# The gated residual of a local-global attention stage, on GpSimd instead of VectorE, with the normalisation one step later

## The chip, the cores and the metric

One core of a Trainium2 chip runs the whole program in one launch. The metric is device microseconds of that core, as a median of runs. Engines: TensorE (PE in the profile; PEld its weight loads), VectorE (DVE), ScalarE (ACT), GpSimd (POOL), SyncE (SP).

## The reference

A decoder of twelve sublayers on x of shape 8 x 256 x 256, each followed by x = layernorm(x + sublayer(x)). The fourth one, a local attention and a global one (over rows compressed four to one) mixed by a gate, is what the change touches. Shortened, it is:

```python
def _L1_attn_ref(x, ...):
    local_x = x[..., :LD]                                   # LD = 128, HH = 8 heads of 16
    lq, lk, lv = split(local_x @ w_lqkv + b_lqkv)
    local_out = _causal_attn(heads(lq), heads(lk), heads(lv)) @ w_lproj + b_lproj
    compressed = x.reshape(Bx, Tc, R * C) @ w_comp + b_comp  # R = 4 rows are one
    gq, gk, gv = split(compressed[..., LD:] @ w_gqkv + b_gqkv)
    global_out = _causal_attn(heads(gq), heads(gk), heads(gv)) @ w_gproj + b_gproj
    global_out = jnp.repeat(global_out, R, axis=1)
    combined = jnp.concatenate([local_out, global_out], axis=-1)
    gate_w = jax.nn.softmax(combined @ w_gate + b_gate, axis=-1)
    return jnp.concatenate([gate_w[..., 0:1] * local_out, gate_w[..., 1:2] * global_out], axis=-1)
...
x = _layernorm(x + _L1_attn_ref(x, ...), axis=-1)
```

## The kernel before

x is held twice in SBUF: x_tok has tokens on the partitions (16 tiles of 128 tokens x 256), x_feat has features on the partitions and feeds the matmuls. A stage is one block in which each engine has its own instruction stream, executed in order; semaphores join them. Everything is f32.

local_global_attention (L1834) works on four groups of two batches (GROUPS = 4, 512 tokens). A group has twelve units of two heads each: eight of local attention (four a batch, 256 tokens; blocks of 128x128 and 128x256 scores) and four of global attention (128 compressed rows, one block a head). The engines follow one hand-written list of steps: `for t in range(STEPS)` runs in each stream, and at_step(t - k, 12, GROUPS) places a piece of work k steps behind the start of its group. Unit u has its scores and minima at step u + 4, its turned probabilities at u + 5, its products at u + 6. So the end of group g (its projection and gate, steps 22 to 28 behind its start) runs beside the units of group g + 1; for group 3 nothing runs beside it.

What each stream does around the gate of group g, by the steps behind the group's start:

- TensorE, in this order in each step: turn_out (L2005; every other step), project_qk (L1909), scores (L1950), turn_back (L2015), compress (L1932, at 6 of a later group; it waits until the x_feat of the group two before it is stored), turn_x (L2043, at 27 and 28, which is batch_turn, L857: four 128x128 transposes of the normalised x_tok), project_v (L1920), output (L2026, at 22 and 23), products (L1983), turn_probs (L1970). The scores of unit u wait for the minima of unit u - 1 and for the normalised output of an earlier pair (out_stored).
- VectorE, in this order in each step: lows (L2204, the masked minima of one unit, side_added), gate_logits (L2250, at 22 and 23), normalise (L2224, every other step), gate_tops (at 24), store_v (L2185), store_probs (L2217), store_back (L2243), gate_shares (L2270, at 25: three small operations), then residual and batch_statistics of the first batch (at 25) and of the second (at 26), then batch_normalise of the first (at 26) and of the second (at 27).
- ScalarE, in this order: batch_store (L867, at 27 and 28: the turned x into x_feat), store_qk (L2079), store_out, store_probs, gates (L2143), store_back, exps (L2110).
- GpSimd: masks at the start, then only batch_power (L841), the power -1/2 of the variances, a 128x2 operation a batch. SyncE issues only loads at the start of the stage.

residual (L2276) is four scalar_tensor_tensor operations a batch, one for each tile of tokens and each half of the features (local, global), x = both * gate + x, where `both` is the ungated output (L2255) and gate a 128x1 column. batch_statistics (L826) is two bn_stats of 128x256, two bn_aggr and one tensor_scalar.

Of the kernel before, what the change touches and what calls it, by code (L numbers as in the profile page):

```python
# [24 lines left out]
P = 128  # L25
# [76 lines left out]
def signals_of_odd_turns(sem):  # L102
# [58 lines left out]
    S.row_loaded_1 = S.masked = sem("odd_row_loaded_1_or_masked")  # L161
    S.row_loaded_2 = sem("odd_row_loaded_2")
    S.row_loaded_3 = sem("odd_row_loaded_3")
# [1670 lines left out]
def local_global_attention(nc, K):  # L1834
# [3 lines left out]
    UNITS, QUADS, EVENTS = GROUPS * SPAN, GROUPS * SPAN // 2, GROUPS * 3  # L1838
    STEPS = (GROUPS - 1) * SPAN + 29
    SM, TB, X, YA, YV, YX = (0, 1), (2, 3), 4, 5, 6, 7  # L1840
# [36 lines left out]
    with turn(nc, K) as block:  # L1877
# [10 lines left out]
        @block.gpsimd  # L1888
        def _(p):
            nc.gpsimd.memset(vh, 0.0).then_inc(S.masks_done, 1)  # L1890
            nc.gpsimd.memset(hide, 0.0).then_inc(S.masks_done, 1)
            nc.gpsimd.memset(gvh, 0.0).then_inc(S.masks_done, 1)
            p.wait_ge(S.masks_done, 3)
            nc.gpsimd.memset(vh[:, :, :, :, HD:HD + 1], 1.0)
            nc.gpsimd.memset(gvh[:, :, HD:HD + 1], 1.0)
            for at in (0, 2 * P, 3 * P):
                ins = nc.gpsimd.affine_select(out=hide[:, at:at + P], in_=hide[:, at:at + P], compare_op=ALU.is_ge,
                                              fill=-MASKED, base=0, pattern=[[-1, P]], channel_multiplier=1)
            ins.then_inc(S.masks_done, 1)
            p.wait_ge(S.masks_done, 4)  # L1900
            paired = hide[:, 3 * P:3 * P + P // 2]
            nc.gpsimd.affine_select(out=paired, in_=paired, compare_op=ALU.is_gt, fill=-MASKED, base=P // 2,
                                    pattern=[[0, P // 2]], channel_multiplier=-1).then_inc(S.masks_done, 1)
            for b in range(B):
                batch_power(nc, p, K, tail, b)

        @block.tensor
        def _(pe):
# [140 lines left out]
            for t in range(STEPS):  # L2049
# [13 lines left out]
                for i in range(2):  # L2063
                    if (g := at_step(t - 27 - i, SPAN, GROUPS)) is not None:
                        turn_x(2 * g + i)
# [12 lines left out]
        def _(a):  # L2078
# [70 lines left out]
            for t in range(STEPS):  # L2149
                for i in range(2):  # L2150
                    if (g := at_step(t - 27 - i, SPAN, GROUPS)) is not None:
                        batch_store(nc.scalar.copy, a, K, 2 * g + i, YX)
# [19 lines left out]
        def _(v):  # L2172
# [97 lines left out]
            def gate_shares(g):  # L2270
                v.wait_ge(S.hid_done, g + 1)
                then(nc.vector.tensor_reduce(total, gate, AX.X, ALU.add))
                then(nc.vector.reciprocal(total, total))
                then(nc.vector.tensor_tensor(gate, gate, spread(total, 2), ALU.mult))

            def residual(b):  # L2276
                for n in range(2):
                    for c in range(2):
                        x = K.x_tok[:, 2 * b + n, c * P:(c + 1) * P]
                        i = 2 * (b % 2) + n  # L2280
                        ins = nc.vector.scalar_tensor_tensor(out=x, in0=both[:, b % 2, n, c * P:(c + 1) * P],
                                                             scalar=gate[:, i, c:c + 1], in1=x, op0=ALU.mult, op1=ALU.add)
                ins.then_inc(S.residual_done, 1)

            for t in range(STEPS):
# [20 lines left out]
                for i in range(2):  # L2306
                    if (g := at_step(t - 25 - i, SPAN, GROUPS)) is not None:
                        residual(2 * g + i)
                        batch_statistics(nc, v, K, tail, 2 * g + i)
                for i in range(2):  # L2310
                    if (g := at_step(t - 26 - i, SPAN, GROUPS)) is not None:
                        batch_normalise(nc, v, K, tail, 2 * g + i)
# [2793 lines left out]
```

## Time and profile before

| what | value |
|---|---|
| median of 3 runs | 2589.14 us (2584.22, 2589.14, 2590.63) |
| the profiled execution, its own time | 2594.83 us |
| its span, first to last instruction | 2593.1 us |
| mean granted TensorE clock | 0.924 of full |
| busy share PE / PEld / DVE / ACT / POOL | 86% / 62% / 54% / 41% / 28% |
| the stage of the change, about | 545 to 759 us of the span |
| the four gates' last operation (L2274) starts at | 627.49, 675.38, 725.54, 750.15 us |

The profiled execution took 1.7 us more than its span, and 5.7 us more than the median of the runs. Busy shares are means over twelve stages with different limits, so they say little of one stage; the timeline around the gates is what shows who waits for whom. In timeline rows a group of equal instructions is merged into one, its second number is the time from the start of the first to the end of the last, and what stands in brackets is how long the engine was idle before it, and who ended that.

### The profile page before, as it was taken

How to read it: one execution, taken by the hardware profiler on the slowest of the kernel's cores; microseconds unless marked ns; L12 is line 12 of the kernel's file. 1: busy time of each engine (PE TensorE's matmuls, PEld its weight loads, DVE VectorE, ACT ScalarE, POOL GpSimd, SP SyncE). 2: the span in 40 equal slices, each digit the busy share in tenths (PEclk: the TensorE clock that was granted, in tenths of full speed). 3: DMA queues.
4: the chain of work that ended last, by engine and by line, in shares of the span. 5: the costliest groups of instructions: out<-in, count | busy, mean ns of one | idle time of the engine just before them, and what ended most of it. 6: DMA issues, size and time to landing. Idle time of an engine off the chain costs nothing. (4 is left out here: it accounts for less than half of the span.)

```text
span 2593.1 us, 37797 instructions
## 1 busy us (share of the span) xinstructions
PE 2218.9 (86%) x12776; PEld 1613.4 (62%) x12776; DVE 1409.6 (54%) x4103; ACT 1060.4 (41%) x2653; POOL 723.4 (28%) x738
## 2 busy tenths in 40 slices
PE   7993599888869959995699799687899799899898
PEld 5772377665547648883388566354465587465687
DVE  3664122256658947757133567544777443777455
ACT  3542111135516620055034166343567543567532
POOL 2323311110004414411634200363534200534111
PEclk9995799979959979996899899899999899999899
DMA  9132211085000010030254301401000000000000
GB/s 235 43 146 103 75 51 44 14 168 43 1 7 1 1 43 1 19 135 7 92 151 129 128 18 29 169 1 33 1 1 1 1 1 1 1 1 1 21 25 21
DMA packets 112237, 127.32 MB, mean 49 GB/s; under 512 B 46515, under 2 KB 100021, under 8 KB 110256
## 3 DMA queue, kind: packets, MB, share of 16 engines
q1 hardware_dynamic: 103312, 103.91, 14.9%
q0 software_dynamic: 8736, 20.99, 2.2%
q8 instruction: 106, 1.74, 0.3%
q14 instruction: 83, 0.68, 0.1%
HBM read 79.93 MB, written 47.90 MB: 49 GB/s over the span
## 5 line engine op out<-in xcount | busy, mean ns | idle before, releaser
L461 PE MATMUL bank<-weights,work 128*128 128x256 f32 (+5 forms) x1768 | 452.4, 393 | 18.8 <-DVE weights L2552 8.1
L461 PE MATMUL bank<-work,weights 128*128 128x256 f32 (+2 forms) x1552 | 392.8, 404 | 19.3 <-DVE work L4794 12.1
L461 PEld LDWEIGHTS bank<-weights,work 128*128 128x128 f32 (+2 forms) x1768 | 318.4, 191 | 101.1 <-issue 49.6
L461 PEld LDWEIGHTS bank<-work,weights 128*128 128x128 f32 x1552 | 293.5, 194 | 91.0 <-DVE work L4794 16.2
L845 POOL TENSOR_TENSOR work<-work,minus_half 128x2 f32<-128x2 f32 x96 | 69.3, 722 | 705.9 <-DVE work L838 705.9
L461 PE MATMUL bank<-weights,x_feat 128*128 128x512 f32 (+2 forms) x576 | 213.6, 505 | 14.8 <-ACT weights L4398 9.1
L870 ACT COPY x_feat<-bank 128x512 f32<-128x512 f32 x80 | 46.6, 585 | 301.8 <-PE bank L862 301.8
L461 PEld LDWEIGHTS bank<-weights,x_feat 128*128 128x128 f32 x576 | 107.4, 199 | 71.8 <-issue 45.9
L4422 ACT ACTIVATE work<-work 128x128 f32<-128x128 f32 (+1 forms) x256 | 137.1, 545 | 0.2
L461 PE MATMUL bank<-x_feat,weights 128*128 128x256 f32 (+3 forms) x400 | 117.7, 472 | 22.1 <-PEq L247 15.2
L1785 DVE TENSOR_TENSOR work<-bank,work 128x384 f32<-128x384 f32 (+1 forms) x64 | 31.4, 491 | 190.6 <-ACT work L1703 190.6
L461 PE MATMUL bank<-weights 128*128 128x256 f32 (+1 forms) x560 | 128.5, 386 | 1.6 <-ACT weights L4441 0.9
L4494 DVE CUSTOM_DVE_ANT_0 work<-bank,work 128x128 f32<-128x128 f32 (+1 forms) x256 | 76.2, 355 | 77.9 <-PE bank L4313 77.5
L461 PEld LDWEIGHTS bank<-weights 128*128 128x128 f32 x560 | 106.8, 196 | 17.0 <-ACT weights L4441 1.4
L461 PE MATMUL bank<-work 128*128 128x256 f32 (+3 forms) x390 | 90.4, 367 | 29.9 <-ACT work L3014 7.8
L461 PEld LDWEIGHTS bank<-x_feat,weights 128*128 128x128 f32 (+1 forms) x400 | 78.4, 214 | 47.6 <-issue 21.1
L862 PE MATMUL bank<-ident,x_tok 128*128 128x128 f32 x320 | 57.4, 311 | 44.9 <-DVE x_tok L853 42.8
L4264 POOL TENSOR_TENSOR work<-work,minus_half 128x8 f32<-128x8 f32 x32 | 52.4, 1637 | 151.3 <-DVE work L4527 151.3
L461 PEld LDWEIGHTS bank<-work 128*128 128x128 f32 (+2 forms) x390 | 66.6, 200 | 44.5 <-issue 12.7
L1603 POOL DMA_INDIRECT rows_back<-work x40 | 38.9, 971 | 196.2 <-DVE work L1793 196.2
L4804 DVE SCALAR_TENSOR_TENSOR work<-bank,weights,work 128x256 f32<-128x256 f32 x96 | 45.5, 481 | 81.3 <-ACT work L4742 80.8
L853 DVE TENSOR_SCALAR x_tok<-x_tok,work 128x256 f32<-128x256 f32 x192 | 80.6, 462 | 14.4 <-POOL work L845 14.2
(461 smaller groups left out, 4503.6 us busy)
## 6 DMA issues: line engine op xcount, KB each, us to landing
weights<-in_weights SPq DMA_DIRECT2D x1, 12296.0 KB, 33.1
weights<-in_weights SPq DMA_DIRECT2D x1, 9360.0 KB, 25.7
weights<-in_weights SPq DMA_DIRECT2D x1, 8488.0 KB, 23.1
work<-rows_in SPq DMA_DIRECT2D x62, 129.0 KB, 2.2
rows_in<-ident SPq DMA_DIRECT2D x2, 3968.0 KB, 43.1
weights<-rows_back SPq DMA_DIRECT2D x8, 768.0 KB, 4.9
work<-rows_in SPq DMA_DIRECT2D x8, 645.0 KB, 4.2
rows_in<-ident SPq DMA_DIRECT2D x2, 2560.0 KB, 33.5
```

The lines of the kernel that those rows point to most:

```text
L461: ins = nc.tensor.matmul(out, lhsT, rhs, start=(i == 0), stop=(i == len(pairs) - 1))
L845: nc.gpsimd.tensor_tensor(t.rstd[:, n, :], t.rstd[:, n, :], K.minus_half[:, 0:2], ALU.pow).then_inc(K.S.rstd_done, 1)
L853: ins = nc.vector.tensor_scalar(x, x, t.mv[:, b % 2, i, 0:1], t.rstd[:, b % 2, i:i + 1], ALU.subtract, ALU.mult)
L862: ins = nc.tensor.transpose(K.bank[bank][:, (2 * k + i) * P:(2 * k + i + 1) * P], K.x_tok[:, 2 * b + i, k * P:(k + 1) * P], K.ident[:])
L870: copy(K.x_feat[:, :, b * L:(b + 1) * L], K.bank[bank][:, :].rearrange("p (k t) -> p k t", k=KT)).then_inc(K.S.xT_stored, 1)
L1603: nc.gpsimd.indirect_dma_start(K.rows_back, bass.IndirectOffsetOnAxis(ap=to, axis=0), y[:, r, :], None, bounds_check=TOP * T - 1, oob_is_e ...
L1785: nc.vector.tensor_tensor(hT[:, q % 2, m, 0:n], K.bank[2 * (at % 2) + 1][:, 0:n], gelu[:, at % 2, 0:n], ALU.mult).then_inc(S.inner_stored, 1)
L4264: nc.gpsimd.tensor_tensor(rk, norm[:, 1, :], K.minus_half[:, 0:H], ALU.pow).then_inc(S.rk_done, 1)
L4422: ins = nc.scalar.activation(probs[:, u % 3, s, at:at + width], probs[:, u % 3, s, at:at + width], ACT.Exp, bias=bias[:, u % 2, i, s:s + 1 ...
L4494: ins = nc.vector.tensor_tensor_reduce(probs[:, u % 3, s, at:at + width], K.bank[SM[s]][:, at:at + width], seen[:, at:at + width], 1.0, -3 ...
L4804: nc.vector.scalar_tensor_tensor(out=hid[rows, b % 2, f, :], in0=K.bank[n % RING][rows, 0:L], scalar=W["b1"][rows, layer, f:f + 1], in1=ge ...
```

## The change

GpSimd gets the residual: for each batch one multiplication of `both` by the gate (128x512 elements, the gate a broadcast operand of 128x4), a wait for itself, and one addition to x_tok (128x512). It waits for gate_stored, a new signal of the last operation of gate_shares. Its power operations of a group stand behind both residuals of that group. On VectorE batch_statistics goes from steps 25 and 26 to 26 and 27, batch_normalise from 26 and 27 to 27 and 28; turn_x on TensorE and batch_store on ScalarE go from 27 and 28 to 28 and 29.

```diff
--- before.py
+++ after.py
@@ -159,7 +159,7 @@
     S.slots_loaded_2 = S.xc_stored = sem("odd_slots_loaded_2_or_xc_stored")
     S.row_loaded_0 = S.sq_stored = sem("odd_row_loaded_0_or_sq_stored")
     S.row_loaded_1 = S.masked = sem("odd_row_loaded_1_or_masked")
-    S.row_loaded_2 = sem("odd_row_loaded_2")
+    S.row_loaded_2 = S.both_scaled = sem("odd_row_loaded_2_or_both_scaled")
     S.row_loaded_3 = sem("odd_row_loaded_3")
     S.row_loaded_4 = sem("odd_row_loaded_4")
     S.row_loaded_5 = sem("odd_row_loaded_5")
@@ -1836,7 +1836,7 @@
     H, HD = 8, 16
     SPAN, LEAD = 12, 4
     UNITS, QUADS, EVENTS = GROUPS * SPAN, GROUPS * SPAN // 2, GROUPS * 3
-    STEPS = (GROUPS - 1) * SPAN + 29
+    STEPS = (GROUPS - 1) * SPAN + 30
     SM, TB, X, YA, YV, YX = (0, 1), (2, 3), 4, 5, 6, 7
 
     qT, kz = A(2, L), A(2, 2, L)
@@ -1901,8 +1901,22 @@
             paired = hide[:, 3 * P:3 * P + P // 2]
             nc.gpsimd.affine_select(out=paired, in_=paired, compare_op=ALU.is_gt, fill=-MASKED, base=P // 2,
                                     pattern=[[0, P // 2]], channel_multiplier=-1).then_inc(S.masks_done, 1)
-            for b in range(B):
-                batch_power(nc, p, K, tail, b)
+
+            def residual(b):
+                i = b % 2
+                parts = both[:, i, :, :].rearrange("p n (c d) -> p (n c) d", c=2)
+                p.wait_ge(S.gate_stored, b // 2 + 1)
+                nc.gpsimd.tensor_tensor(parts, parts, gate[:, 2 * i:2 * i + 2, :].rearrange("p n c -> p (n c)").unsqueeze(2)
+                                        .broadcast_to([P, 4, P]), ALU.mult).then_inc(S.both_scaled, 1)
+                p.wait_ge(S.both_scaled, b + 1)
+                x2 = K.x_tok[:, 2 * b:2 * b + 2, :]
+                nc.gpsimd.tensor_tensor(x2, x2, both[:, i, :, :], ALU.add).then_inc(S.residual_done, 1)
+
+            for g in range(GROUPS):
+                residual(2 * g)
+                residual(2 * g + 1)
+                batch_power(nc, p, K, tail, 2 * g)
+                batch_power(nc, p, K, tail, 2 * g + 1)
 
         @block.tensor
         def _(pe):
@@ -2061,7 +2075,7 @@
                 if (g := at_step(t - 6, SPAN, GROUPS)) is not None:
                     compress(g)
                 for i in range(2):
-                    if (g := at_step(t - 27 - i, SPAN, GROUPS)) is not None:
+                    if (g := at_step(t - 28 - i, SPAN, GROUPS)) is not None:
                         turn_x(2 * g + i)
                 for i in range(2):
                     if (g := at_step(t - 4 * i - 1, SPAN, GROUPS)) is not None:
@@ -2148,7 +2162,7 @@
 
             for t in range(STEPS):
                 for i in range(2):
-                    if (g := at_step(t - 27 - i, SPAN, GROUPS)) is not None:
+                    if (g := at_step(t - 28 - i, SPAN, GROUPS)) is not None:
                         batch_store(nc.scalar.copy, a, K, 2 * g + i, YX)
                 if (g := at_step(t - 8, SPAN, GROUPS)) is not None:
                     store_global(g)
@@ -2271,16 +2285,7 @@
                 v.wait_ge(S.hid_done, g + 1)
                 then(nc.vector.tensor_reduce(total, gate, AX.X, ALU.add))
                 then(nc.vector.reciprocal(total, total))
-                then(nc.vector.tensor_tensor(gate, gate, spread(total, 2), ALU.mult))
-
-            def residual(b):
-                for n in range(2):
-                    for c in range(2):
-                        x = K.x_tok[:, 2 * b + n, c * P:(c + 1) * P]
-                        i = 2 * (b % 2) + n
-                        ins = nc.vector.scalar_tensor_tensor(out=x, in0=both[:, b % 2, n, c * P:(c + 1) * P],
-                                                             scalar=gate[:, i, c:c + 1], in1=x, op0=ALU.mult, op1=ALU.add)
-                ins.then_inc(S.residual_done, 1)
+                nc.vector.tensor_tensor(gate, gate, spread(total, 2), ALU.mult).then_inc(S.gate_stored, 1)
 
             for t in range(STEPS):
                 if (u := at_step(t - LEAD, 1, UNITS)) is not None:
@@ -2304,11 +2309,10 @@
                 if (g := at_step(t - 25, SPAN, GROUPS)) is not None:
                     gate_shares(g)
                 for i in range(2):
-                    if (g := at_step(t - 25 - i, SPAN, GROUPS)) is not None:
-                        residual(2 * g + i)
+                    if (g := at_step(t - 26 - i, SPAN, GROUPS)) is not None:
                         batch_statistics(nc, v, K, tail, 2 * g + i)
                 for i in range(2):
-                    if (g := at_step(t - 26 - i, SPAN, GROUPS)) is not None:
+                    if (g := at_step(t - 27 - i, SPAN, GROUPS)) is not None:
                         batch_normalise(nc, v, K, tail, 2 * g + i)
```

## Rows read from the trace of the kernel before

**Rows 1.** Windows: stretch, its us, busy PE, PEld, DVE, ACT, POOL, PEclk, DMA, GB/s.

```profile
633.00:636.00 3.00, 2.10 (x11) 1.41 (x12) 1.69 (x11) 0.85 (x2) 0.78 (x1) 0.50 0.00 0
```

**Rows 2.** Timeline, first gate: start us, us, engine line op out<-in [idle before <-releaser].

```profile
627.49 0.17 DVE L2274 TENSOR_TENSOR work<-work 128x8 f32<-128x8 f32 x1
...
627.70 1.14 DVE L2281 SCALAR_TENSOR_TENSOR x_tok<-work,x_tok 128x128 f32<-128x128 f32 x4
...
628.87 0.75 DVE L831 BATCH_NORM_STATS2 work<-x_tok 128x6 f32<-128x256 f32 x2
...
629.94 0.17 DVE L838 TENSOR_SCALAR work<-work 128x2 f32<-128x2 f32 x1
...
630.30 0.28 DVE L2212 CUSTOM_DVE_ANT_0 work<-bank,work 128x128 f32<-128x128 f32 x1
...
630.51 0.28 DVE L2222 COPY work<-bank 128x128 f32<-128x128 f32 x1
...
630.70 0.41 PE L2011 MATMUL bank<-ident,work 128*128 128x128 f32 x2 [2.55 <-issue]
...
633.90 1.09 PE L862 MATMUL bank<-ident,x_tok 128*128 128x128 f32 x4 [2.38 <-DVE x_tok L853]
...
634.37 0.35 DVE L2238 TENSOR_TENSOR work<-bank,work 128x64 f32<-128x64 f32 x2
...
637.82 1.56 PE L1967 MATMUL bank<-work 32*128 32x128 f32 x8
...
639.60 0.60 PE L862 MATMUL bank<-ident,x_tok 128*128 128x128 f32 x4
...
642.28 1.52 ACT L2115 ACTIVATE work<-work 128x128 f32<-128x128 f32 x4
...
643.86 0.88 PE L1979 MATMUL bank<-ident,work 128*128 128x128 f32 x6 [0.99 <-ACT work L2115]
...
645.52 3.92 PE L461 MATMUL bank<-x_feat,weights 128*128 128x128 f32 x16
```

**Rows 3.** Timeline, same columns, second gate (first row) and third gate.

```profile
681.79 1.09 PE L862 MATMUL bank<-ident,x_tok 128*128 128x128 f32 x4 [2.38 <-DVE x_tok L853]
...
725.54 0.17 DVE L2274 TENSOR_TENSOR work<-work 128x8 f32<-128x8 f32 x1
...
735.35 1.09 PE L862 MATMUL bank<-ident,x_tok 128*128 128x128 f32 x4
...
740.07 0.47 PE L2023 MATMUL bank<-ident,work 128*128 128x128 f32 x1 [0.53 <-DVE work L2238]
```

**Rows 4.** Timeline, same columns, fourth gate and the end of the stage.

```profile
750.15 0.17 DVE L2274 TENSOR_TENSOR work<-work 128x8 f32<-128x8 f32 x1
...
754.98 0.73 DVE L853 TENSOR_SCALAR x_tok<-x_tok,work 128x256 f32<-128x256 f32 x2
...
755.86 1.09 PE L862 MATMUL bank<-ident,x_tok 128*128 128x128 f32 x4 [9.64 <-DVE x_tok L853]
```

**Rows 5.** GpSimd elsewhere: timeline of two dependent operations, one line's min/median/max ns.

```profile
1820.55 1.26 POOL L4267 TENSOR_TENSOR work<-work 128x512 f32<-128x512 f32 x1
1821.96 1.04 POOL L4271 TENSOR_TENSOR work<-work 128x512 f32<-128x512 f32 x1
...
L3911 POOL TENSOR_TENSOR x_tok<-x_tok,weights x8: 1257/1446/1530, 1662.6 to 1764.7; 128x512 f32<-128x512 f32 x8
```

**Rows 6.** Timeline, another stage: L4076 beside a GpSimd operation, and alone.

```profile
1662.57 1.26 POOL L3911 TENSOR_TENSOR x_tok<-x_tok,weights 128x512 f32<-128x512 f32 x1
1662.68 1.70 DVE L4076 TENSOR_TENSOR work<-weights,work 128x512 f32<-128x512 f32 x1
...
1665.22 0.69 DVE L4076 TENSOR_TENSOR work<-weights,work 128x512 f32<-128x512 f32 x1
```

**Rows 7.** Timeline: the scores behind the gate logits, first and third gate.

```profile
621.92 0.49 PE L1967 MATMUL bank<-work 32*128 32x128 f32 x4 [1.43 <-DVE work L2238]
...
717.63 0.79 PE L1967 MATMUL bank<-work 32*128 32x128 f32 x4 [2.29 <-DVE work L2238]
```

## The prediction

> **What bounds the kernel now.** I read the page first: TensorE is the busiest engine over the span, but that is a mean over twelve stages. I then took the timeline around each gate, following TensorE's idle time and what ended it; after that the windows, for the granted clock, and last GpSimd's groups in other stages, for prices.
>
> In the first gate the gate is ready at 627.66 us (627.49 + 0.17). VectorE then runs the residual and the statistics of one batch before the minima of unit 22 may start, near 630.1. TensorE stood idle 2.55 us for those minima; after its scores it stood idle 2.38 us more for the normalised x_tok, because turn_x stands ahead of products in its queue [rows 2]. The trace calls the first of the two "issue", but what it waited for is side_added, and it started 0.12 us after the last of the minima (630.30 + 0.28). The granted clock then was at 0.50, the lower level (1.2 GHz) [rows 1], and the scores of unit 24 took 1.56 us. The second gate repeats this, with 2.38 us ahead of turn_x [rows 3]. The third has no scores to feed after its first steps, and the fourth nothing beside it: there the chain gate, residual, statistics, power, normalisation, turning is the path itself, and TensorE was idle 9.64 us before it [rows 4]. So the stage has two bounds: in gates 1 and 2 VectorE's order, which holds TensorE; at the end, the length of the chain.
>
> **Part by part.** *Removed from VectorE:* 4 operations a batch, 1.14 us [rows 2], eight times. *Added to GpSimd:* two operations a batch. The stage has no such row. The nearest are two dependent 128x512 operations of another stage: 1.26 us with two full operands, then after a 0.15 us wait for itself 1.04 us with a broadcast operand, as the gate is here [rows 5]. So a residual is 1.04 + 0.15 + 1.26 = 2.45 us, two are 4.90, and the batch's power operation stands behind both. *Bounds:* additions to x_tok took 1.257 to 1.530 us [rows 5]; with 1.53 for both operations a residual is 3.2 us, and with 1.04 for both 2.2. I keep 2.45, from the nearest forms. The wait for the gate gets 0.1 us (TensorE started 0.12 us behind the minima that it waited for).
>
> *The step moved.* First gate, instruction by instruction. GpSimd: first residual 627.76 to 630.21, second to 632.66, both powers behind it. VectorE: minima 22 (0.49) to 628.15, store_probs (0.28) to 628.45 [rows 2]; it then waits for GpSimd until 630.25. Behind that wait stand the minima 23, the normalised output and store_probs, and TensorE's scores 24 wait for them. Statistics, from the start of bn_stats to the end of the last one, are 628.87 to 630.11, that is 1.24 us: to 631.49. Minima 23 to 631.98; the normalised output, about 0.6 (its second half is 0.35), to 632.6; store_probs to 632.9 [rows 2]; statistics of the second batch to 634.1 (its residual is in at 632.66, so no wait); normalisation 0.73 [rows 4] to 634.85. TensorE meanwhile does the scores 23, products 21, turned probabilities 22 and project_qk with nothing in their way, until some 630.9; scores 24 at 632.65; turn_x at 634.97 (0.12 us behind the normalisation).
>
> In the kernel before, the turning that follows scores 24 started at 639.60, and the turned probabilities of unit 24 at 643.86, with ScalarE's copy, store_qk, stores and exponentials between them (exponentials from 642.28) [rows 2]: 4.26 us. The same sequence stands behind the turning in the new kernel, so the turned probabilities start at 634.97 + 4.26 = 639.23. **Gain of the gate: 643.86 - 639.23 = 4.6 us.** The second turning comes at about 637.6, in TensorE's idle time. The compression at 645.52 needs both turnings stored; it moves to some 641, behind the second copy. From there on TensorE is the bound, so the gain stays. The second gate is the same: 4.6.
>
> Third gate: gate ready at 725.71; the same walk puts the first normalisation's end at 732.9 and the turning at 733.0 to 734.1 at the low clock. Products and turned probabilities (some 1.2) end at 735.3, store_probs, store_back and normalisation (0.28 + 0.28 + 0.73) at 736.65; the second turning, 1.09 us, at 737.85 (before: 736.44) [rows 3]. Before, the products of the last unit also came behind it, but waited for a copy of their probabilities that now is long there; I get 739.9 for the turning of the last output against 740.07. **Gain 0.2 us.**
>
> Fourth gate, all on the path: gate at 750.32, both residuals in at 750.32 + 0.1 + 4.90 = 755.32; VectorE's statistics of the second batch stand ahead of the first normalisation, so that ends at 755.32 + 0.04 + 1.24 + 0.73 = 757.33, against 754.98 + 0.73 = 755.71 before [rows 4]. The two turnings and copies follow as before. **Loss 1.6 us.** The step that the loops are longer, the semaphore under a second name and the wait saved behind gate_shares cost nothing: no engine has work in them. SyncE's and GpSimd's queues are passed by no DMA of this stage. The cover of GpSimd's work is the minima and stores of units 22 and 23; in the fourth gate it is gone, which is the 1.6.
>
> **Sum:** -4.6 - 4.6 - 0.2 + 1.6 = -7.8 us: 2594.8 becomes 2587.0 by the profiled execution, which is 5.7 above the median of the runs; on the median, 2589.1 - 7.8 = 2581.3. In general each 0.1 us on the mean price of a GpSimd operation (1.225 with the wait) costs 0.4 us in each of the four gates, 1.6 in all.
>
> A rule against the change is in the Trainium skill, "GPSIMD Engine Reference", section Engine selection: elementwise work on a tile belongs on VectorE, GpSimd being about twice slower with two inputs. By the rule, twice VectorE's 0.69 us of a 128x512 operation [rows 6] is 1.38 for each, the mean with the wait 1.455, and the sum -7.8 + 3.7 = -4.1. Of the rows, 1.26 is near it and 1.04, the broadcast form, is not.
>
> **The rivals.**
>
> A. The walk as above, -7.8, with some 1.5 to either side for its small terms. 0.50.
>
> B. The clock. In the third gate the granted clock also fell: there TensorE had idled 2.29 us for the logits, and the scores took 0.79 us where the same ones of the first gate, behind 1.43 us of idle, took 0.49. From those scores to the last gate operation it was 725.54 - 717.63 = 7.91 us, against 627.49 - 621.92 = 5.57 [rows 2, 3, 7]. If earlier work shifted by 9 us keeps it high there, 2.3 more are gained: -10.1. For: the falls follow recent idle time, which changes. Against: those 2.29 us of idle stay. 0.20.
>
> C. The clock falls in the gates all the same. TensorE's new idle stretches are about 1.7 and 1.1 us, with 1.2 of work between; the rows have one case behind 1.43 with the clock up and one behind 2.29 with it down [rows 7]. At the low level the turning is 1.09 for 0.60 and scores 1.56 [rows 2], and about 2 us of each gain go: -3.6. 0.16.
>
> D. GpSimd and VectorE hold each other up. L4076 took 1.70 us beside a GpSimd operation and 0.69 alone [rows 6]. If the statistics did so, each would end about 1 us later: -7.8 + 2 x 4 x 0.8, about -1.5. Against: L4076 has two full operands in SBUF, and what runs beside the residuals has one (bn_stats), or takes the other from PSUM (minima). 0.09.
>
> The Trainium skill, "SBUF — State Buffer", section Who interferes with whom, has that rule: a VectorE operation with two SBUF inputs and a GpSimd one that reads SBUF exclude each other, the later one waiting fully. The rows on L4076 agree; by it nothing beside the residuals is held, and D does not happen.
>
> E. Slower. GpSimd's price decides: at 1.225 + 7.8/16 = 1.71 us a mean operation the sum is zero, and at 2.2 it is +7.8. The place is VectorE's wait for residual_done in statistics, with minima and output behind it, and the last gate's chain. It needs the 4x128 broadcast from 128x4, or x_tok beside busy engines, to cost 1 us more than any row of the size: 1.53 is the highest [rows 5]. 0.05.
>
> That the change does not do what it says I leave out: the signals and the buffers' reuse (both, gate) hold, and every old wait on residual_done is met long before.
>
> **How the numbers follow.** A measurement of this kernel can tell about 0.3% from no change, 7.8 us, which lies in the middle of A. A gives 0.26 to faster and 0.24 to no change; B 0.20 to faster; C 0.15 and D 0.09 to no change, C's last 0.01 to faster; E 0.04 slower and 0.01 no change, and slower gets 0.01 of A's no change for what I overlooked. Faster 0.47, no change 0.48, slower 0.05. The time is A's, 2581.3. The range takes in A, B to its lower side (2575), C (2585.5) and D (2587.6), with 1 us for the runs' own spread: 2574 to 2589.
>
> **What would show it.** In the first gate: GpSimd's two operations at 1.04 and 1.26 us, first residual in 2.5 us behind the gate; the minima 22 some 2 us earlier; TensorE's 2.55 us wait gone, its turning at 7.3 us behind the gate and the compression some 4.5 us nearer to the gate than 17.9 us. In the last gate the turning 1.6 us further from it (7.1 for 5.5). Wrong would be: a GpSimd operation over 1.5 us; statistics stretched beside it; the same distance from gate to compression, which would mean that another wait holds TensorE; or half clock between scores 24 and the compression.

## The result and the profile after

The changed kernel takes 2591.63 us (median of 22 runs, 2588.12 to 2594.4) against 2588.44 (22 runs, 2582.18 to 2591.68): ratio 1.0014, 95% interval 1.0008 to 1.002. It is 0.14% slower, within what was called no change, but 10 us above the forecast of 2581.3 and outside the range. Measured again beside the experiments (e9 below), the ratio was 0.9997 (0.9984 to 1.001), so that the changed kernel is slower at all is not settled; that it brings far less than the forecast 7.8 us is (0.9984 would be 4.1).

GpSimd behaves as priced: the two operations take 1.04 and 1.26 us (eight of each within 13 ns), the first residual is in 2.5 us behind the gate (625.02 - 622.55), and the 2.55 us wait of [rows 2] is gone. The timeline of the changed kernel's first gate, VectorE, GpSimd and TensorE rows (columns as in [rows 2]):

```profile
622.38 0.17 DVE L2288 TENSOR_TENSOR work<-work 128x8 f32<-128x8 f32 x1
...
622.63 1.04 POOL L1909 TENSOR_TENSOR work<-work 128x512 f32<-128x512 f32 x1 [76.25 <-DVE work L2288]
...
623.75 1.27 POOL L1913 TENSOR_TENSOR x_tok<-x_tok,work 128x512 f32<-128x512 f32 x1
...
625.06 0.75 DVE L831 BATCH_NORM_STATS2 work<-x_tok 128x6 f32<-128x256 f32 x2 [1.69 <-POOL x_tok L1913]
...
626.11 1.26 POOL L1913 TENSOR_TENSOR x_tok<-x_tok,work 128x512 f32<-128x512 f32 x1
626.13 1.26 DVE L838 TENSOR_SCALAR work<-work 128x2 f32<-128x2 f32 x1
627.31 0.28 DVE L2226 CUSTOM_DVE_ANT_0 work<-bank,work 128x128 f32<-128x128 f32 x1
...
628.50 0.92 PE L1981 MATMUL bank<-work 32*128 32x128 f32 x8 [2.95 <-DVE work L2252]
...
629.53 0.17 DVE L838 TENSOR_SCALAR work<-work 128x2 f32<-128x2 f32 x1
...
630.48 1.09 PE L862 MATMUL bank<-ident,x_tok 128*128 128x128 f32 x4 [0.69 <-DVE x_tok L853]
...
632.90 1.65 PE L1981 MATMUL bank<-work 32*128 32x128 f32 x8
```

The row to see is L838, the addition of epsilon to two numbers a lane. It took 0.17 us in [rows 2] and takes 1.26 here: it starts 0.02 us behind GpSimd's addition L1913 and ends with it. Behind it stand the minima (L2226) and the normalised output (L2252), behind those TensorE's scores, idle 2.95 us. The second batch's L838, with GpSimd idle, takes 0.17 again. Over the four gates (minimum, median, maximum ns):

```profile
L838 DVE TENSOR_SCALAR work<-work x8: 168/714/1266, 626.1 to 749.3; 128x2 f32<-128x2 f32 x8
```

The clock falls as well. Windows of the same gate (columns as in [rows 1]):

```profile
626.00:630.00 4.00, 1.29 (x10) 0.75 (x10) 3.86 (x19) 0.69 (x2) 2.21 (x4) 1.00 0.00 0
630.00:633.50 3.50, 3.02 (x16) 2.01 (x18) 2.14 (x13) 1.90 (x6) 0.56 (x1) 0.56 0.00 0
633.50:637.00 3.50, 3.50 (x19) 2.24 (x17) 2.38 (x13) 2.27 (x7) 0.00 (x0) 0.50 0.00 0
```

In the last gate, where [rows 4] had the turning 5.54 us behind the gate (750.32 to 755.86), it now comes 6.85 behind (743.38 to 750.23):

```profile
743.45 1.04 POOL L1909 TENSOR_TENSOR work<-work 128x512 f32<-128x512 f32 x1 [16.88 <-DVE work L2288]
744.57 1.26 POOL L1913 TENSOR_TENSOR x_tok<-x_tok,work 128x512 f32<-128x512 f32 x1
745.79 1.04 POOL L1909 TENSOR_TENSOR work<-work 128x512 f32<-128x512 f32 x1
...
746.94 1.26 DVE L838 TENSOR_SCALAR work<-work 128x2 f32<-128x2 f32 x1
...
750.23 1.08 PE L862 MATMUL bank<-ident,x_tok 128*128 128x128 f32 x4 [10.96 <-DVE x_tok L853]
```

Where the stage's time went, in us, each number a difference of two rows' times (a gate is ready when its last operation ends):

| | before | changed |
|---|---|---|
| start of the stage's first compression to gate 1 | 79.40 | 79.16 |
| gate 1 to its first turning / to the compression | 6.24 / 17.86 | 7.93 / 16.17 |
| gate 1 to gate 2 | 47.89 | 48.88 |
| gate 2 to its first turning / to the compression | 6.24 / 17.80 | 8.00 / 17.50 |
| gate 2 to gate 3 | 50.16 | 47.14 |
| gate 3 to gate 4 | 24.61 | 24.81 |
| gate 4 to its first turning | 5.54 | 6.85 |
| the stage, between GpSimd's marks (L253) | 210.67 | 209.91 |
| the last stretch, mark to mark, untouched by the change | 185.24 | 187.55 |

Gate 1 gave 1.69 us (17.86 - 16.17) instead of 4.6. Then 48.88 is 2.68 more than the 46.20 (47.89 - 1.69) that this gain alone would leave, and gate 3 comes 2.72 sooner than gate 2's 0.30 explains (50.16 - 0.30 - 47.14). The two nearly cancel: the clock now falls ahead of gate 2 and stays up ahead of gate 3. TensorE's scores are the sign. Ahead of gate 2 the scores behind the gate logits still take 0.49 us (663.01), but the next unit's take 0.80 (666.62) where the kernel before has 0.49 (672.47). Ahead of gate 3 the scores behind the logits (713.29) take 0.49 where [rows 7] had 0.79, behind the same 2.29 us of idle. The low clock that starts ahead of gate 2 lasts until 20 us behind it, which is why gate 2 gains only 0.30. Timeline of TensorE in the changed kernel, ahead of gates 2 and 3, and the windows ahead of and behind gate 2 (671.42):

```profile
663.01 0.49 PE L1981 MATMUL bank<-work 32*128 32x128 f32 x4 [1.43 <-DVE work L2252]
...
666.62 0.80 PE L1981 MATMUL bank<-work 32*128 32x128 f32 x4
...
713.29 0.49 PE L1981 MATMUL bank<-work 32*128 32x128 f32 x4 [2.29 <-DVE work L2252]
```

```profile
664.60:671.40 6.80, 6.80 (x36) 4.49 (x34) 2.89 (x15) 2.56 (x9) 0.00 (x0) 0.50 0.00 0
671.40:691.80 20.40, 19.62 (x89) 13.40 (x89) 11.86 (x59) 8.38 (x24) 6.07 (x6) 0.50 0.01 2
```

So the stage gains 0.76 us and the last stretch loses 2.31. The spans of the two profiled executions are the other way round (2590.1 against 2593.1 us), because their first two stretches, ahead of the change, differ by 4.9 us; over the sixteen profiled executions below, the first lasted 211.5 to 218.0 us and the second 325.9 to 328.5, whatever the kernel. Therefore I compare stages by their marks, and kernels by their runs.

### The profile page after: what moved, and what is told of

Read it like the earlier page. It is cut to its first block and busy times, and to the rows that moved or that the text cites. A ratio compares the mean times of both kernels' runs of the same rounds, so it can differ in the third digit from the quotient of the medians.

```text
span 2590.1 us, 37781 instructions
## 1 busy us (share of the span) xinstructions
PE 2216.9 (86%) x12776; PEld 1614.8 (62%) x12776; DVE 1406.7 (54%) x4071; ACT 1060.3 (41%) x2653; POOL 742.8 (29%) x754
## 5 line engine op out<-in xcount | busy, mean ns | idle before, releaser
L461 PE MATMUL bank<-work,weights 128*128 128x256 f32 (+2 forms) x1552 | 392.2, 404 | 20.1 <-DVE work L4798 12.6
L461 PEld LDWEIGHTS bank<-work 128*128 128x128 f32 (+2 forms) x390 | 66.1, 198 | 43.8 <-issue 12.6
```

The source lines that it names most:

```text
L461: ins = nc.tensor.matmul(out, lhsT, rhs, start=(i == 0), stop=(i == len(pairs) - 1))
```

## The experiments

A time below is the median of a kernel's own runs. The kernel before was run beside each batch of experiments, with medians of 2591.11 us (e1, e3 to e5), 2593.17 (e6 to e9), 2592.42 (e10 to e13) and 2592.28 (e14, e15), so times of different batches should not be subtracted. The ratios, each to the kernel before of the same batch, can be compared, within their intervals.

**The epsilon operation.** e1 is the changed kernel with epsilon added by GpSimd, behind both residuals:

```diff
+                p.wait_ge(S.mean_done, b + 1)
+                nc.gpsimd.tensor_tensor(tail.rstd[:, n, :], tail.mv[:, n, :, 1], eps, ALU.add).then_inc(S.var_done, 1)
                 batch_power(nc, p, K, tail, b)
```

> The changed kernel, but in this stage GpSimd adds the epsilon to the variances (two elements a partition) ahead of the power; VectorE's tensor_scalar is gone. Theory Port (GpSimd's addition to x_tok holds that tensor_scalar, 1.26 us in place of 0.17 in all four gates): the minima of unit 23 start about 1.1 us earlier behind the gate (3.7 in place of 4.8 us), no VectorE operation beside the additions is stretched, the first turning is about 1.1 us nearer to the gate in gates 1 to 3 and 0.1 to 0.3 in gate 4, and the time is 2 to 3 us under the changed kernel, level with the kernel before. Theory Clock (what TensorE loses in the gates is the granted clock): the same local shift, but the time moves by under 1 us from the changed kernel's.

Measured: 2583.46 us (12 runs), ratio to the kernel before 0.9978 (0.9965 to 0.999). The wait ahead of the scores falls from 2.95 to 1.65 us, turning at 6.65 and compression at 12.61 us behind gates 1 and 2, the clock at 1.00 through both, the stage 200.67 us. Timeline and windows of its first gate (626.63):

```profile
629.13 0.75 DVE L846 BATCH_NORM_STATS2 work<-x_tok 128x6 f32<-128x256 f32 x2 [1.68 <-POOL x_tok L1927]
...
630.17 1.26 POOL L1927 TENSOR_TENSOR x_tok<-x_tok,work 128x512 f32<-128x512 f32 x1
...
631.28 0.92 PE L2001 MATMUL bank<-work 32*128 32x128 f32 x8 [1.65 <-DVE work L2272]
631.40 0.19 POOL L1932 TENSOR_TENSOR work<-work 128x2 f32<-128x2 f32 x1
```

```profile
626.00:633.00 7.00, 4.79 (x36) 2.68 (x34) 4.97 (x28) 2.69 (x10) 5.76 (x8) 1.00 0.02 5
633.00:640.00 7.00, 6.13 (x49) 4.33 (x50) 5.33 (x30) 6.04 (x17) 0.69 (x1) 1.00 0.00 0
```

With this one small operation elsewhere, a gate gives 5.2 us (17.8 - 12.6), a little more than the 4.6 forecast. The operation's price came as theory Port had it; the gain of the stage (9.2 us under the changed kernel's) was far more than the 2 to 3 us expected of the time, and the clock, at 1.00 here, goes with it. That alone doesn't say whether the wait counts or something else in e1.

**The same wait, put back.** e6 is e1 with three bn_stats (1.05 us, results unused) behind the first batch's moments:

```diff
+                        for k in range(0 if i else 3):
+                            nc.vector.bn_stats(junk[:, 8 * k:8 * k + 6], K.x_tok[:, 4 * g, :])
```

> The kernel with the epsilon on GpSimd, and on VectorE three more bn_stats of 128x256 (0.37 us each, 1.1 us, results unused) behind the moments of each group's first batch, where the held tensor_scalar cost 1.1 us in the changed kernel. Theory Held (the 1.1 us of VectorE ahead of the minima of unit 23 are what cost the gates their gain, by the clock that falls behind the longer idle of TensorE): the first turning comes 7.7 to 7.9 us behind the gate in place of 6.7, the granted clock falls to 0.50 behind it, the compression stands at about 16.2 us in place of 12.6, and the time is 5 to 9 us above the kernel with the epsilon on GpSimd. Theory Other (the epsilon's move helped in some other way): turning later by 1.1 us, but the clock stays up and the time rises by 2 to 3 us only.

Measured: 2590.06 us (12), 0.999 (0.9979 to 1.0002). The scores wait 2.61 us, the compression is back at 15.66, the stage at 208.12. TensorE's row and the windows of its first gate (623.72):

```profile
629.33 0.92 PE L2001 MATMUL bank<-work 32*128 32x128 f32 x8 [2.61 <-DVE work L2272]
```

```profile
628.00:631.00 3.00, 1.29 (x10) 0.75 (x10) 2.93 (x17) 0.69 (x2) 1.91 (x5) 1.00 0.00 0
631.00:634.50 3.50, 3.41 (x19) 2.04 (x19) 2.18 (x12) 2.68 (x8) 0.49 (x1) 0.57 0.00 0
```

One microsecond of wait costs 3.05 us to the compression (15.66 - 12.61), because the clock falls with it, as theory Held had it. The stage is 7.4 us longer than e1's. The ratios differ by 0.0012, some 3 us, and their intervals overlap; the 5 to 9 us expected of the time are not shown.

**What is held.** e10 and e11 leave the epsilon operation on VectorE in another form, at its place: e10 as a reduction over the variance and a stored epsilon (one operand), e11 as an addition of two operands.

```diff
-    nc.vector.tensor_scalar(t.rstd[:, n, :], t.mv[:, n, :, 1], LN_EPS, None, ALU.add).then_inc(S.var_done, 1)
+    nc.vector.tensor_reduce(t.rstd[:, n, :], t.mv[:, n, :, 1:3], AX.X, ALU.add).then_inc(S.var_done, 1)    # e10
+    nc.vector.tensor_tensor(t.rstd[:, n, :], t.mv[:, n, :, 1], t.eps, ALU.add).then_inc(S.var_done, 1)     # e11
```

> The changed kernel; the epsilon is still added on VectorE in this stage and at the same place, but by a tensor_reduce over the variance and a constant beside it (one SBUF input) in place of the tensor_scalar. Theory Form (only the form tensor_scalar is held by a GpSimd addition, because it takes the ports that the two engines share): 0.17 to 0.2 us in place of 1.26, first turning 6.6 to 6.8 us behind the gate in gates 1 to 3 in place of 7.9, clock at 1.00 through the gate where it was up ahead of it, gate to compression 12.6 us, and 5 to 8 us under the changed kernel. Theory Any (whatever VectorE reads or writes there, a small operation right behind the start of a GpSimd addition is held): 1.2 us again and the changed kernel's time.

> The changed kernel; the epsilon is added on VectorE by a tensor_tensor of the variances and a constant tile (two SBUF inputs). Theory Form in the skill's wording (two SBUF inputs share the read port with GpSimd): held as the tensor_scalar was, 1.2 us, first turning 7.9 us behind the gate, and the changed kernel's time within 2 us. Rival (only tensor_scalar is held): 0.2 us, turning at 6.7, time as the kernel with the reduction.

The operation's row in e10 and in e11 (minimum, median, maximum ns):

```profile
L855 DVE TENSOR_REDUCE work<-work x8: 157/157/158, 628.6 to 746.1; 128x2 f32<-128x4 f32 x8
```

```profile
L855 DVE TENSOR_TENSOR work<-work x8: 161/706/1257, 628.6 to 751.7; 128x2 f32<-128x2 f32 x8
```

e10: 2588.62 us (12), 0.9982 (0.997 to 0.9993), stage 204.40. e11: 2591.32 us (12), 0.9992 (0.9981 to 1.0003), stage 209.92, every distance within 0.1 us of the changed kernel's. So the form decides: at one place, with one output of 128x2, the addition of two operands is held and the reduction is not. The two stages differ by 5.5 us, which is what the hold costs here. But e10's gates don't reach e1's 12.6: the scores start 4.94 us behind the gate, after 1.94 us of idle, and the clock falls all the same, 7.9 us behind gate 1 and 7.0 behind gate 2 (compression at 15.25 and 15.21; 12.6 was expected). Window of e10's first gate (625.00):

```profile
632.90:639.70 6.80, 6.80 (x33) 4.88 (x35) 3.53 (x16) 5.21 (x16) 0.00 (x0) 0.50 0.00 0
```

**The move alone.** e3 is the kernel before with the step moved and the residual still on VectorE:

```diff
-                        residual(2 * g + i)
-                        batch_statistics(nc, v, K, tail, 2 * g + i)
+                        residual(2 * g + i)
+                for i in range(2):
+                    if (g := at_step(t - 26 - i, SPAN, GROUPS)) is not None:
+                        batch_statistics(nc, v, K, tail, 2 * g + i)
```

(normalisation, turning and its store one step later, as in the change)

> The kernel before with the residual still on VectorE at steps 25 and 26, and statistics, normalisation, turning and storing one step later as in the change. Theory Order (the gates gain because turning stands behind the next unit's products, and not because GpSimd relieves VectorE): from gate to compression about 16.2 us as in the changed kernel (17.9 before), the last gate's chain only 0.2 us longer than before (5.7 us from gate to turning, 6.9 in the changed kernel), and the time 1 to 3 us under both kernels. Theory Relief (VectorE's 2.3 us a gate matter): from gate to compression 17 us or more, and the time at or above that of before.

Measured: 2585.02 us (9), 0.9973 (0.9963 to 0.9983); stage 203.33, compression at 15.45 and 15.32, last turning 5.29 behind its gate. The move gives more than the whole change (7.3 us of the stage against 0.8), though the clock still falls in its gates. Theory Order holds, with more gained than it expected.

**The clock.** e4 is the changed kernel and e5 the kernel before, with transposes of the identity, whose results nothing uses, in TensorE's waits around the gates. The core of both:

```diff
+            def fill(n):
+                for _ in range(n):
+                    nc.tensor.transpose(K.bank[YX][:, 0:P], K.ident[:], K.ident[:])
```

e4 calls it with 8 (14 for the third gate) ahead of the scores behind the gate logits, 4 ahead of turn_x and 16 at step 28; e5 with the same 8 and 14, 15 at step 27 and 14 ahead of turn_x.

> The changed kernel with transposes of the identity into an unused bank put where TensorE waits in gates 1 to 3: 8 or 14 ahead of the scores behind the gate logits, 16 ahead of the scores of the second step behind the wait, 4 ahead of the first turning. Theory Clock: the granted clock stays at 1.00 through gates 1 to 3, from gate to compression it takes about 14.5 us in place of 16.2, second gate to third gate no longer than first to second, and the time is 4 to 6 us under the changed kernel. Theory Port alone: the stretches keep their lengths, since what ends TensorE's waits is VectorE, and the time is within 1 us of the changed kernel's.

> The kernel before with the same kind of transposes where TensorE waits: 8 or 14 ahead of the scores behind the gate logits, 15 ahead of the turned output that waits for the minima, 14 ahead of the first turning. Theory Clock: granted clock 1.00 through gates 1 to 3, from gate to compression about 15.5 us in place of 17.9, and the time 4 to 6 us under the kernel before; the changed kernel filled in the same way then lies within 2 us of this one, and the difference of the two unfilled kernels is one of the clock. Theory Port: this one gains nothing, or the same kernels' order stays as it was (changed one 3 us above).

e5: 2581.77 us (6), 0.9961 (0.9947 to 0.9976), the fastest of all; clock at 1.00 through three gates, compression at 15.43 in gates 1 and 2, stage 200.44, so the low clock cost the kernel before some 10.2 us in this stage (210.67 - 200.44). e4: 2589.1 us (12), 0.9988 (0.9979 to 0.9998); the fill keeps the clock ahead of gate 2 (gate 1 to gate 2 46.21, just the 46.20 worked out above) and in gate 2 (compression 13.89), but in gates 1 and 3 it falls as before (16.16 in gate 1). So the expected full clock through three gates was missed; the stage is 203.57 us. Gate 2 is the useful one, for it has the held operation and the full clock: 13.89, between the 16.2 of the changed kernel's first gate and e1's 12.61. Of the 3.6 us between those two, 2.3 are the clock and 1.3 the held operation. Filled, the two kernels are not within 2 us, as was expected, but 7.3 apart. Windows of e4 in gate 1 (623.92), then ahead of and in gate 2 (670.13):

```profile
631.00:637.00 6.00, 5.75 (x31) 3.84 (x30) 3.97 (x22) 3.58 (x11) 0.79 (x1) 0.56 0.00 0
...
661.00:669.00 8.00, 7.40 (x63) 5.31 (x59) 6.43 (x34) 4.85 (x15) 0.00 (x0) 1.00 0.00 0
670.00:678.00 8.00, 6.48 (x52) 4.70 (x48) 6.11 (x28) 2.19 (x8) 5.93 (x6) 1.00 0.01 2
```

**The last gate.** e7 is e1 with the last group's residual back on VectorE; e8 is e7 with e4's transposes, 8 (14 for the third gate) ahead of the scores behind the gate logits and 8 at step 28 of the first two.

```diff
+                            v.wait_ge(S.gate_stored, GROUPS)
+                            residual(2 * g + i)
+                            batch_statistics(nc, v, K, tail, 2 * g + i)
```

> The kernel with the epsilon on GpSimd, and the residual, statistics and epsilon of the last group (two batches) on VectorE as before the change. The last gate's chain has nothing beside it: from gate to turning 5.5 to 5.7 us in place of 6.6, the rest of the stage unchanged, time 1.0 to 1.3 us under the kernel with the epsilon on GpSimd. Rival: the end of the stage is set by something else, and the time stays.

> The kernel with the epsilon on GpSimd and the last residual on VectorE, with transposes of the identity into an unused bank where TensorE waits: 8 or 14 ahead of the scores behind the gate logits, 8 ahead of the scores behind the held minima in the first two gates. Theory Clock: no fall of the granted clock from the first gate to the third one, gate to gate 43.2 us or less twice (44.2 and 43.6 before), and the time 1 to 4 us under the same kernel without them. Rival: the waits are now short enough, and the time is the same within 1 us.

e7: 2585.35 us (12), 0.9973 (0.996 to 0.9985); last turning at 5.54 again, 1.10 less than e1's 6.64, yet the stage is 203.15, because the clock was low ahead of gate 1 and in it (80.68 and 16.66). Up to the last group e7's program is e1's, so this fall comes with an edit to later work, or by chance; with one profile of each I can't tell. e8: 2586.1 us (12), 0.9977 (0.9964 to 0.999); the shortest stage of all, 195.04, 8.1 us under e7's, and the stretch behind it is 3.9 shorter too, but the profiled executions last as long (2579.62 and 2579.45): the last stretch, at 188.39, is 3.0 us longer than e7's, and the seven stretches between 8.9 longer together. I have no cause for it.

**Is it chance?** e9 and e13 are the changed kernel again, e12 the kernel before again.

> The changed kernel once more, on the chip of the others. The distances from gate to first turning are the same to 0.1 us (7.9, 8.0, 7.9, 6.9), VectorE's held tensor_scalar is 1.26 us again in all four gates. Theory Clock (the falls of the clock outside the waits are by chance): gate to gate differs by 1 to 3 us from 48.9 and 47.1, and the stage from 209.9. If these repeat to 0.3 us, the falls belong to the kernel. The time is 0 to 5 us above the kernel before and 7 to 11 above the one with the epsilon on GpSimd.

> The kernel before, once more. The local distances repeat (gate to first turning 6.2, 6.2, 6.2 and 5.5 us, gate to compression 17.8). Theory Chance (falls of the clock outside the held waits differ by run): gate to gate differs by up to 3 us from 47.9 and 50.2, and the stage lies between 207 and 213 us (210.7 in the first profile). If it repeats to 0.3 us, the clock's pattern belongs to the kernel.

> The changed kernel, third profile. Local distances 7.9, 8.0, 7.9, 6.9 us and 1.26 us of held tensor_scalar; the stage between 206 and 211 us (209.9 and 207.0 so far). The last stage, which the change does not touch, takes 187.5 us as in both earlier profiles of this kernel if that belongs to the kernel, or 185.2 as in the kernel before if it is chance.

e9: 2592.34 us (12), 0.9997 (0.9984 to 1.001). e13: 2595.78 and e12: 2593.06, one run each. The distances of the gates repeat to 0.1 us in all three, fall of the clock ahead of gate 2 included, but for one: e9's clock was low until 10 us behind gate 2 and not until 20, so its compression came 2.9 us sooner (14.58, stage 207.01). The last stretch took 187.53 and 187.60 us in the changed kernel, 185.21 in the kernel before.

**The last stretch.** Up to here it took 187.5 us wherever the last turning was 6.85 us or more behind its gate, and 185.2 to 185.4 at 6.65 or less, e8 aside. So I moved the last gate alone: e14 is the changed kernel with the last group's residual back on VectorE; e15 the kernel before with four unused bn_stats ahead of the last gate's statistics:

```diff
+                        if g == GROUPS - 1 and i == 0:
+                            v.wait_ge(S.residual_done, 2 * g + 1)
+                            for j in range(4):
+                                nc.vector.bn_stats(tail.spare[:, j, :], K.x_tok[:, 4 * g, :])
```

> The changed kernel with the residual of the last gate alone back on VectorE, in its four operations a batch; the first three gates stay as changed. Theory, that the last gate's longer wait tips the clock pattern of the stage behind it: the last turning comes back to 5.5 us behind the gate logits, the stage of the change ends 1.3 us earlier, and the last stage takes 185.2 us in place of 187.5; the time is some 3.6 us below the changed kernel's, about 0.2 to 1 us from the kernel before (ratio 0.999 to 1.000). Rival, that the last stage's pattern comes from what the changed kernel does earlier (the clock in its second and third gates): the last stage stays at 187.5 us, and only 1.3 us are gained. The first three gates are as in the changed kernel either way: turning 7.9 us behind the gate, epsilon operation 0.7 to 1.26 us.

> The kernel before with four more bn_stats of 0.35 us ahead of the statistics of the first batch in the last gate, whose results nothing uses, so that the last turning comes 1.4 us later, at 6.9 us behind the gate logits. Theory, that this delay tips the stage behind it: the last stage takes 187.5 us in place of 185.2, and the time is 3.7 us above the kernel before (ratio 1.0014), as in the changed kernel, though no gate's residual is on GpSimd. Rival: the last stage stays at 185.2 us and the time is only 1.4 us higher (1.0005). The first three gates stay at 6.24 us from gate to turning.

Measured: e14 2588.41 us (10), 0.9991 (0.9976 to 1.0007), last turning 5.54, stage 208.58, last stretch still 187.32. e15 2589.24 us (10), 0.9994 (0.9978 to 1.0011), last turning 6.85, stage 211.88, last stretch still 185.25. The theory fell in both. What differs in that stretch is the clock. Windows at its start, in the changed kernel and in the kernel before, on the same work:

```profile
2398.62:2402.00 3.38, 2.77 (x9) 2.42 (x10) 1.10 (x1) 1.62 (x6) 0.59 (x2) 0.50 0.02 7
2402.00:2405.50 3.50, 3.50 (x10) 2.77 (x9) 0.00 (x0) 1.35 (x6) 0.00 (x0) 0.53 0.00 0
```

```profile
2403.90:2407.30 3.40, 2.79 (x9) 2.44 (x10) 1.10 (x1) 1.64 (x6) 0.59 (x2) 0.50 0.02 5
2407.30:2410.80 3.50, 3.50 (x22) 2.58 (x21) 0.69 (x1) 1.33 (x6) 0.00 (x0) 1.00 0.00 0
```

In the second window of each the low clock gets through ten matmuls, the full one through 22. Both clocks fall at the same work; only the return differs. That is not the whole of it: in e14, as slow there, the clock is back as early as in the kernel before, and it is low further on, from 2428.4 to 2445.3 us, for longer than there. What in a stage 1,600 us earlier decides it, I couldn't find.

## Why the prediction was wrong

- **GpSimd's prices** were right: 1.04 and 1.26 us, a residual in 2.5 us behind the gate as forecast. Between two dependent operations the gap was 0.08 us, not 0.15. The factor of two over VectorE of the Trainium skill, "GPSIMD Engine Reference", Engine selection (1.38 us) was too high here: 1.5 and 1.8 times the 0.69 us.
- **"Statistics … that is 1.24 us"** was the step that failed. They were priced from a row with GpSimd idle and set beside GpSimd's addition. They took 2.33 us (625.06 to 627.39), and scores 24 started 5.95 us behind the gate instead of 4.99. Rival D had the mechanism, with 0.09 and against the wrong operands: I looked for two large operands in SBUF, and the operation held has two numbers a lane. I cited the Trainium skill, "SBUF — State Buffer", section Who interferes with whom, for two-input operations alone and wrote that by it nothing is held. The same section says that copy, cast and tensor_scalar can also take the port pair that VectorE shares with GpSimd, and that whoever issues first keeps the other out for its whole instruction, while tensor_reduce never contends on trn2. e10 (0.157 us) and e11 (up to 1.257) agree on the forms, and in each held row GpSimd had started first; no row here has VectorE first. The trace of the kernel before had the case too, just ahead of [rows 6]: a tensor_scalar took 0.65 us beside a GpSimd memset, and ended with it, and 0.18 alone. Its rows:

```profile
1661.23 1.38 POOL L3904 MEMSET work<- 128x1536 f32 x1 [2.84 <-POOLq L247]
...
1662.00 0.65 DVE L4075 TENSOR_SCALAR work<-work 128x32 f32<-128x32 f32 x1
...
1665.01 0.18 DVE L4075 TENSOR_SCALAR work<-work 128x32 f32<-128x32 f32 x1
```

- **The full clock between scores 24 and the compression**, which the 4.6 us took as given, failed too, and not with the hold alone; it is rival C (0.16). e10 is the kernel that the walk described: nothing held, scores 24 at 4.94 us (4.99 forecast). It gave 2.6 us (17.86 - 15.25) and not 4.6, because the clock fell there as well. e1 and e6 show the tie: with 1.65 us of wait the clock stays at 1.00 and a gate gives 5.2 us (e7's first gate, where it had fallen ahead of the gate, aside); with 2.61 it falls and 3.05 of them go. C's own size, 2 us a gate, was near: gate 1 gave 2.9 us less than forecast (1.69 for 4.6), 0.9 of it by the hold (15.25 to 16.17) and 2 where the clock fell without it. The order of work in walk A was right; its instruction times were those of the full clock.
- **Rival B** was half right. The fall ahead of the third gate went (-2.72), as it said, but one came ahead of the second (+2.68), with the same 1.43 us of idle as [rows 7] had with the clock up; and the 2.29 us ahead of gate 3 now leave it up. So the wait just ahead of the scores doesn't decide by its length alone. I had weighed the falls of the kernel before only, and no new one.
- **The last gate** lost 1.31 us, forecast 1.6: the smaller gaps in GpSimd (0.08 for 0.15, twice) and shorter waits between the engines. L838's hold cost nothing there: it ends with GpSimd's second addition, which VectorE waits for in any case, and e10, without the hold, has the same 6.85. **The third** lost 0.20 where 0.2 was to be gained.
- **The last stretch** cost 2.31 us that no term held. With the stage's -0.76 it makes +1.6 of the +3.2 us between the medians; the other half lies within what the untouched stretches vary, and I can't place it.
- **Smaller slips**, which decided nothing. Each 0.1 us on a GpSimd operation was said to cost 0.4 us in every gate, but in the walk of gates 1 and 2 scores 24 wait for the first residual alone, two operations and not four, as long as the second residual is in before VectorE asks for it. Loads of this stage do pass SyncE's queue, but in the windows of the gates the DMA engines move next to nothing (a share of 0.01 at most). And rival E asked for 1 us above the highest row, 1.53, where its own 2.2, less the wait, is 0.6 above it.

Why 7.8 us of expected gain became 0.8 is settled for the stage: the held epsilon operation, the clock that falls in the gates, and a fall of the clock that changed its gate. Of the 7.0 us that are missing, the hold with the falls that follow it is 5.5 (e11 against e10), and the other 1.5 is what e10, with nothing held, lacks of the forecast (6.3 for 7.8). What moves the clock's falls from one gate to another is not shown. The last stretch's slower form stands in three profiles of the changed kernel and in e4, e10, e11 and e14, in none of the kernel before, e3, e5 or e15, nor in e1, e6 and e7 (185.24 to 185.35), which have GpSimd's residuals too; its cause is open.

## What to carry to other kernels

Before work moves to GpSimd, list what VectorE will run beside it, form by form: a tensor_scalar or a two-operand operation on two numbers was held until GpSimd's ended (1.26 us), a reduction (0.157 us) or bn_stats (0.75 us for two, as alone) was not. Then ask whether TensorE's wait behind it grows or shrinks; here one microsecond of it was worth three. And try the parts of a change singly: moving the step alone (0.9973), or the whole change with epsilon on GpSimd too (0.9978), beat the kernel before with intervals wholly below 1. These two are not told apart by the time, though their stages took 203.3 and 200.7 us.

## What I had not expected of the hardware

- A 0.17 us operation on 128x2 numbers was held to 1.26 us in all of the four gates, and GpSimd's addition was not longer for it (1.26 us).
- Most of the clock's falls repeat with the program: the same distances to 0.1 us in three executions of the changed kernel, and the last stretch 185.2 to 185.4 or 187.3 to 187.6 us by kernel in fifteen of sixteen. Not all do: e9's gate 2 is one exception, and the seventh stretch took 183.9 us in two executions of the changed kernel and 186.8 in the third (e13). A difference of 2 to 3 us in one stretch of two profiles is therefore weak evidence until it is repeated.
- Adding matmuls that nothing uses made the kernel before 0.39% faster (e5).
